# Two score weight matmul groups of the next pass issued inside the last message block, in a two-layer graph network on one Trainium2 core

## What is computed

```python
w_m = (efeat @ W_msg + b_msg).reshape(E, in_f, -1)      # 16 x 16 per edge
w_a = (efeat @ W_attn + b_attn).reshape(E, in_f, -1)
h_src = feat[src][:, :, None]
e1 = w_m * h_src
e2 = w_a * h_src
seg_max = jax.ops.segment_max(e2, dst, num_segments=N)
ex = jnp.exp(e2 - seg_max[dst])
denom = jax.ops.segment_sum(ex, dst, num_segments=N)
attn = ex / denom[dst]
ft = jax.ops.segment_sum(e1 * attn, dst, num_segments=N)
return ft.sum(axis=1)
```

## Time and profile before

| | |
|---|---|
| median of 3 runs | 6410.05 us (6404.79 to 6413.98) |
| the profiled execution | 6405.31 us |
| its span, first to last instruction | 6403.6 us |
| VectorE busy | 3554.8 us (56%) |
| TensorE busy | 2752.5 us (43%) |
| GpSimd busy | 4012.1 us (63%) |
| mean granted TensorE clock | 0.710 of full speed |

### The profile page before, as it was taken

One profiled execution on the slowest core, in us unless ns is written; L12 is line 12 of the kernel. 1 busy time (PEld: TensorE's weight loads), 2 busy tenths in 40 slices (PEclk: granted clock), 3 DMA queues, 4 the chain that ended last, 5 costly groups with the idle time before them and its releaser, 6 DMA issues.

```text
span 6403.6 us, 57451 instructions
## 1 busy us (share of the span) xinstructions
PE 2752.5 (43%) x13527; PEld 1931.1 (30%) x13528; DVE 3554.8 (56%) x4214; ACT 1211.0 (19%) x1559; POOL 4012.1 (63%) x3713
## 2 busy tenths in 40 slices
PE   3530000000000000000367788777778788778777
PEld 1110000000000000000145555555556555556555
DVE  8321112121222122233468888888888888888887
ACT  3440000000000000000122222222222222222222
POOL 0325766767676676675466666666666666677663
PEclk9965555555555555555678888988888888888888
DMA  5861111111111111111000001001001011011110
GB/s 159 270 212 18 20 26 26 23 31 25 28 33 27 27 30 30 33 39 31 20 13 20 20 20 28 20 20 27 21 20 28 20 28 28 20 28 28 28 28 18
DMA packets 157958, 251.68 MB, mean 39 GB/s; under 512 B 73726, under 2 KB 130563, under 8 KB 145156
## 3 DMA queue, kind: packets, MB, share of 16 engines
q0 software_dynamic: 126192, 100.10, 8.0%
q1 hardware_dynamic: 31711, 151.31, 7.1%
q10 hardware_dynamic: 32, 0.01, 0.0%
HBM read 113.57 MB, written 136.63 MB: 39 GB/s over the span
## 4 chain that ended last, share of the span: by engine, by line
PE 22%; issue 21%; DVEq 18%; POOL 16%; DVE 14%; DMA 5%; another core or an unknown queue 2%; POOLq 1%; ACT 1%; SPq 0%; ACTq 0%
POOL gath L350 15%; PE psS L555 8%; PE psS L560 7%; DVEq L1193 5%; PE psW L549 4%; DMA table<-arena 3%; DVE stage L1154 3%; DVEq L1161 3%; DVE stage L1196 2%; DVEq L1121 2%; DVE work L756 1%; DVE arena L1154 1%; DVEq L1154 1%; POOL info_dram L321 1%
## 5 line engine op out<-in xcount | busy, mean ns | idle before, releaser
L350 POOL DMA_INDIRECT gath<-h_dram,hidx x1695 | 1961.2, 1157 | 1051.3 <-issue 550.1
L350 POOL DMA_INDIRECT gath<-table,blkidx x1646 | 1621.2, 985 | 535.8 <-issue 506.4
L543 PE MATMUL psT<-identb,stage 128*100 128x128 bf16 x2448 | 228.0, 252 | 2530.0 <-issue 2461.4
L560 PE MATMUL psS<-stage,ident 128*128 128x256 f32 x3390 | 936.0, 432 | 166.6 <-DVE stage L1196 161.0
L543 PEld LDWEIGHTS psT<-identb,stage 128*100 128x100 bf16 x2448 | 204.6, 152 | 2568.6 <-issue 2528.8
L555 PE MATMUL psS<-arena,ident 128*128 128x256 f32 x3390 | 829.1, 382 | 0.2 <-issue 0.2
L1154 DVE TENSOR_TENSOR arena<-psW,gath 128x768 f32 (+1 forms) x565 | 522.4, 952 | 529.9 <-DMA gath<-h_dram,hidx 293.5
L560 PEld LDWEIGHTS psS<-stage,ident 128*128 128x128 f32 x3390 | 710.6, 217 | 320.7 <-DVE stage L1196 199.0
L549 PE MATMUL psW<-wst,stage 100*128 100x256 bf16 x3390 | 577.1, 291 | 308.4 <-DVE arena L1154 171.5
L555 PEld LDWEIGHTS psS<-arena,ident 128*128 128x128 f32 x3390 | 605.4, 191 | 70.4 <-issue 0.4
L692 ACT ACTIVATE arena<-arena 128x1536 f32<-128x1536 f32 (+1 forms) x294 | 421.8, 1435 | 984.9 <-DVE arena L1183 983.7
(11 more groups left out here) (222 smaller groups left out, 2478.0 us busy)
## 6 DMA issues: line engine op xcount, KB each, us to landing
table<-arena SPq DMA_DIRECT2D x50, 1610.0 KB
ef<-arena SPq DMA_DIRECT2D x50, 805.7 KB
gath<-h_dram,hidx POOLq DMA_INDIRECT x1695
gath<-table,blkidx POOLq DMA_INDIRECT x1646
arena<-in_edge_attr SPq DMA_DIRECT2D x50, 257.8 KB
table<-arena SPq DMA_DIRECT2D x50, 186.9 KB
arena<-first_dram POOLq DMA_DIRECT2D x1, 915.5 KB, 13.7
info<-info_dram POOLq DMA_DIRECT2D x2, 432.0 KB, 6.4
```

The costliest lines, as they stand in the source:

```text
L350: pool.indirect_dma_start(out=gath[:, q, s, :], out_offset=None, in_=rows, in_offset=bass.IndirectOffsetOnAxis(ap=idx[:, q, s:s + 1].bitca ...
L543: last = nc.tensor.transpose(psTb[0:KE, t % 2, j, 0:GP], efs[:, 8 * t + j, :], identb[0:GP, 0:GP])
L560: nc.tensor.matmul(psS[0:GP, IO:2 * IO], ident[0:GP, 0:GP], prod[:, c0:c0 + IO], start=False, stop=False)
```

## The change

A new function `first_weights` waits for the first copied group of transposed features of pass w and issues the weights of its half-blocks 0 and 1. It is called once before the loop for pass 0, and then for pass k + 1 in the last message block of pass k, after that block's transposes and ahead of its wait for `q_ready`. Since nb is known at run time only, blocks 2 to 6 each have a branch (`nb < b + 2`) that tests whether the block is the last. The loop over half-blocks in a pass now begins at h = 2, and the exponent sums that follow weights h are those of half-block h - 2. Nothing is changed on the other engines, and the number of matmuls is the same.

```diff
+            def first_weights(w, q, at0):
+                pe.wait_ge(m["efT_sb"], w * (S // 8) + 3)
+                for h in range(2):
+                    weights(0, q, h, at0)
+
...
             for t in range(S // 8):
                 transposes(0, t)
+            first_weights(0, 0, 0)
...
-                    for h in range(NHW):
+                    for h in range(2, NHW + 2):
                         if h < MINH:
                             weights(0, q, h, tb * 4)
-                        else:
+                        elif h < NHW:
                             with pe.If(nh > h):
                                 weights(0, q, h, tb * 4)
-                        with pe.If(prev > h):
-                            exp_sums(1 - q, h)
+                        with pe.If(prev > h - 2):
+                            exp_sums(1 - q, h - 2)
...
                         with pe.If(nb > b):
+                            if b == NBW - 1:
+                                first_weights(k + 1, 1 - q, (tb + nb) * 4)
+                            elif b >= MINB - 1:
+                                with pe.If(nb < b + 2):
+                                    first_weights(k + 1, 1 - q, (tb + nb) * 4)
                             pe.wait_ge(m["q_ready"], tb + (b + 1))
                             prod_sums(2 * b)
```

## The result

The changed kernel takes 6425.08 us (median of 17 runs, 6411.8 to 6441.26), the kernel before beside it on the same chip 6410.05 (17 runs, 6404.79 to 6419.65). The ratio is 1.0023, 95% interval 1.0016 to 1.003: slower by about 15 us, where 98 less had been forecast.

A forecast was written before the change was run, and what follows sets the result against it. VectorE was taken to pace L1, with its standstill at seams between passes to be won. Late passes 72.6, early 25 and pass 1 0.7 sum to 98 us less: 6312 us, range 6278 to 6365, chance 0.70.

The forecast's parts named there:

- New branches. I count 0: TensorE's message blocks: 144 added jumps, each 0.07 to 0.33 us, taken to lie ahead of a wait and cost nothing.
- The upper bound named for this part, 48: Cost in us if all 144 added jumps were exposed at the largest branch value, 0.33.
- the early term, 25: Seams of passes 2 to 23: 25 us gained, the middle between 45 at full clock and 6 at half clock.
- The late term, 72.6: Seams of passes 24 to 49: 48.8 us from 15 with early gathers plus 23.8 from 11 at a gather floor.
- Both floors: Seams: VectorE can run half-blocks 0 and 1 without loss; gathers hold L1165 to 4.23 us after rows are there.
- T + 3.22: New L1165 time after a pass's last L1196 where gathers are early; T is when first weights are issued now.
- rival D: Seams: the first weights don't come early, held by features, w_free or transposes; no change, 6410; chance 0.03.
- A: Rival: early passes give nothing, TensorE's lower clock spreads, half of late gather-floor gain lost; 61 less, 6349; chance 0.10.
- B: Rival: gathers become the bound in late passes too, 1.5 us later in 26 seams; 59 less, 6351; chance 0.07.
- C: Rival: finish (L1115) waits for exponent sums in 22 early passes at half clock; 62 slower, 6472; chance 0.04.
- E: Rival: all at full clock, 128 less, 6282; chance 0.06. In "E + 1.3", E is the end of a pass's last L1196.
- the signs named ahead: Right: first half-blocks early, late psW waits about halved from 132 us; wrong: finish waits, late L1165 or gathers, longer branches.

The follow-up runs named there:

- compact form: `compact`: the changed kernel with its last message block taken out of the unrolled blocks and written once, place in a register; 6123.49 us, ratio 0.9921 to the kernel before.
- The padding: Never-entered weights instructions put in TensorE's loop; in the kernel before 6272.35 against 6169.87 us, ratio 1.0167.
- compact_pad: The compact form with the longer never-entered part added in TensorE's loop; 6175.16 us, ratio 1.001 to the kernel before.

## Why the prediction was wrong

Forecast 98 us less, measured 15 more: 113 are to be explained. The two traces of the changed kernel and the kernel before, on the chip of the forecast, are 34 apart instead of 15, so on them it is 132. By their parts, in us (the rest of a pass runs from its first subtraction to its last L1196):

| after less before | measured | forecast |
|---|---|---|
| passes 24 to 49: seams, scores, rest | 12.3, 6.8, 2.0 | -72.6, 0, 0 |
| passes 2 to 23: seams, scores, rest | -5.9, 9.5, 0.0 | -25, 0, 0 |
| pass 1 | 0.9 | -0.7 |
| all ahead of pass 1 | 8.1 | 0 |
| behind pass 49 | 0.2 | 0 |

- **The step that failed first is "New branches. I count 0".** It priced the branch instructions (their median is still 0.068) and not the code that comes with them. Six copies of `first_weights` and five branches in each of two unrolled passes lengthen the loop by 160 instructions (150 compiled), past the bound of 1735 to 1745. In the changed kernel itself the even late seams, those with a jump back, lie 80.5 above their forecast and the odd ones 4.5; in the compact form, without fetches and on another chip, the same even seams take 91.9, below the 93.2 forecast. The padding prices the fetch at 52 us in the compact form (`compact_pad` against `compact`) and at 102 in the kernel before. The upper bound named for this part, 48, came from the wrong mechanism.
- **The rule of the Trainium skill, too.** The largest branch of the earlier trace rows, 0.33, shows no fetch, and the closing branch of the kernel before, 0.2, doesn't either. The page Runtime: NRT & Kernel Launch, section Instruction fetch mechanics, says that a taken branch out of the prefetched code waits for a fetch. The prediction asked that only of the added branches. In the changed kernel the rule holds at a branch that the diff doesn't touch, the jump back over the whole loop: 4.0 in the median. At the added branches the trace still doesn't agree with it. The test "does the largest branch of before show a stall" could not answer, since the loop of before still fitted.
- **The second step is the early term, 25.** The prediction named the mechanism, and its bound, L1165 at 6.1 after the first half-block, is what most seams show (6.12 in 16 of 22). On the chip of the forecast the seams gain 5.9, the 6 that the prediction gave for the low clock everywhere; but their scores lose 9.5, which wasn't costed, so the term is a loss of 3.6. The low clock should have been the expected case. On the chip of the compact form the loss is larger, 16.6 in the seams and 7.6 in the scores, since there the seams of the kernel before take 276.5, not 306.4: its first maximum comes 4.23 after the first half-block, the distance of full clock, in 10 of 22 seams, against 2 of 22 on the first chip. Why the chips differ in this was not found.
- **The late term, 72.6, holds where nothing is fetched.** Compact form: 75.4. In part that is luck: apart from passes 48 and 49 single seams lie up to 1.5 below their forecast and up to 1.4 above it, and this cancels. Both floors hold with it: half-blocks 0 and 1 begin at E + 1.3, and the gather-floored seams lie at 7.3 to 7.5 (7.35 forecast) in ten passes. Passes 48 and 49 miss most, 10.1 where T + 3.22 gives 7.5 and 8.0. Their four message blocks are over before ScalarE has copied the features for the early weights, for which TensorE stands 2.09 into pass 48, and the last sums are pushed behind them: rival D, in two seams.
- **Sum.** Of the 132 between the traces the late passes make up 93.7 (80.5 of them in the even seams), the early ones 28.6. Of the remaining 10, 8 lie ahead of pass 1 and weren't assigned. In pass 1 the finish waits 8 longer than before; with that the rest of the pass is 5.8 longer, its seam is 4.9 shorter, and 0.9 are lost where 0.7 were forecast as a gain.
- **Rivals.** A had a right place for the early passes (25 forecast away, 28.6 measured), but its other half, 12 off the late gather-floored seams, does not show in the compact form. B fell: into passes 17 and 23 the first half-block still begins 5.6 to 5.7 after E. C, the slower case, fell: the finish waits for TensorE only in two passes, pass 1 and behind the last. E fell, since the low clock stayed. The sign came from a mechanism that none of them held. The two waits of the finish (the kernel before has two as well, together 22.0, the longer 14.3):

```profile
DVE work L1126 <- remote: 16.1, 1, 16.1
DVE work L1126 <- PE psS L568: 14.6, 1, 14.6
```

Of the signs named ahead, the late waits for TensorE (137.2, not half of 132) and the longer branches (one of 350 took 1.05, 0.33 before) spoke against the forecast; the first two half-blocks at E + 1.3 spoke for its mechanism.

## What to carry to other kernels

Count a change in instructions of the loop as well as in work. Where a loop of an engine is unrolled to well over a thousand instructions, read the packets of its instruction queue and the time of the branch that closes the loop, before and after. Code that must run in one of several unrolled places is better factored out with a register as its index than copied behind branches, and if something must be duplicated, duplicate the operation with the fewest instructions. When work is moved ahead of a wait, ask what is left for the engine to do in that wait: here two groups of sums in a 3.4 us stand decided over the clock of the next ones.

## What the runs showed of the hardware

- The bound is narrow, but not sharp: up to 1735 instructions in the list of TensorE's loop (1628 compiled), 8 packets in the whole run; at 1745 (1652), 125 packets, nine at each of 13 jumps back and none at the 11 others; at 1771 to 1867 (1662 to 1760), 204 to 224.
- The fetch at a jump back took 3.8 to 5.0 us in the median and up to 6.6 to 7.8, and it costs only where TensorE's path sets the pace: in the compact form nothing in the 22 early seams, 50 in the 26 late ones.
- Padding of 1771 instructions cost 146 us, of 1867 102. A longer loop isn't always the dearer one.
